# Where two normalisations and a cosine product run in a transformer layer on one NeuronCore

## The reference

```python
x = x + _layernorm(_L0_attn_ref(_layernorm(x), Wq, bq, Wk, bk, Wv, bv, Wo, bo))
x = x + _layernorm(_L0_ffn_ref(_layernorm(x), gate_w, up_w, down_w, gate_s, up_s, down_s))
# attention: 32 heads of 16 channels; queries and keys get a rotary embedding,
# q * cos + rotate_half(q) * sin, twice (position and coarse time); causal softmax
# feed-forward: down((silu(gate(x) * gate_s) * (up(x) * up_s))) * down_s, 1408 wide, ternary weights
```

## Time and profile before

| What | Value |
|---|---|
| time, median of 3 runs | 2977.47 us (2976.86 to 2978.34) |
| time of the profiled execution | 2972.66 us |
| its span, from first to last instruction | 2970.9 us |
| mean granted clock of PE | 0.961 |
| busy in the span: PE, DVE, ACT, POOL | 2555.1, 2219.8, 1325.7, 1034.1 us |

### The profile page before, as it was taken

One profiled execution on the slowest core, in us unless ns is written; L12 is line 12 of the kernel. 1 busy time (PEld: TensorE's weight loads), 2 busy tenths in 40 slices (PEclk: granted clock), 3 DMA queues, 4 the chain that ended last, 5 costly groups with the idle time before them and its releaser, 6 DMA issues. The chain is left out here.

```text
span 2970.9 us, 58497 instructions
## 1 busy us (share of the span) xinstructions
PE 2555.1 (86%) x19584; PEld 1229.0 (41%) x19584; DVE 2219.8 (75%) x6495; ACT 1325.7 (45%) x1710; POOL 1034.1 (35%) x1051
## 2 busy tenths in 40 slices
PE   3788888888888888888888888708999999999997
PEld 1344443444443444434444444204444444444443
DVE  5899899889898898898898999573554555455544
ACT  2465555556555555555555555432222222222221
POOL 3456365365464663653654655210000000000000
PEclk9999999999999999999999999859999999999999
DMA  4232332332332323323323323040111111111111
GB/s 151 85 88 76 97 105 74 110 98 73 105 93 74 109 73 99 105 70 112 100 72 105 99 68 108 30 177 15 43 71 42 56 42 71 42 56 48 65 42 43
DMA packets 125363, 237.31 MB, mean 80 GB/s; under 512 B 11440, under 2 KB 94896, under 8 KB 111920
## 3 DMA queue, kind: packets, MB, share of 16 engines
q1 hardware_dynamic: 123056, 232.84, 24.8%
q10 hardware_dynamic: 2048, 1.05, 0.1%
HBM read 148.39 MB, written 84.41 MB: 78 GB/s over the span
## 5 line engine op out<-in xcount | busy, mean ns | idle before, releaser
L674 DVE CUSTOM_DVE_ANT_0 mx<-mx,causal 128x512 f32<-128x512 f32 (+3 forms) x2048 | 942.9, 517 | 99.5 <-PE mx L799 98.6
L518 ACT ACTIVATE probs<-ts,exp_scale 128x1024 f32<-128x1024 f32 x640 | 713.1, 1114 | 656.5 <-PE ts L813 536.1
L444 POOL TENSOR_SCALAR_AFFINE_SELECT probs<-probs 128x512 f32<-128x512 f32 x512 | 326.3, 655 | 691.0 <-ACT probs L518 691.0
L1219 DVE SCALAR_TENSOR_TENSOR hidden<-gu,up_scale,silu 128x512 f32<-128x512 f32 x176 | 131.9, 749 | 417.9 <-PE gu L1269 408.0
L1078 ACT ACTIVATE silu<-gu,gate_scale 128x512 f32<-128x512 f32 x176 | 121.0, 688 | 631.2 <-PE gu L1269 631.2
L1053 POOL TENSOR_TENSOR f_rstd<-f_var,f_neg_half 128x4 f32<-128x4 f32 x32 | 32.3, 1010 | 929.1 <-DVE f_var L1196 647.5
L799 PE MATMUL mx<-kT,qT 64*128 64x512 f16 (+3 forms) x2048 | 256.1, 308 | 69.5 <-issue 51.2
L1267 PE MATMUL gu<-f_xT_hi,gate_hi 128*128 128x512 f16 x704 | 267.9, 381 | 52.0 <-issue 52.0
L827 PE MATMUL xb<-probs,vs 128*32 128x512 f32 (+3 forms) x4096 | 308.8, 443 | 1.6 <-POOL probs L444 1.1
L674 DVE DVE_READ_ACCUMULATOR2_ANT row_max<- 128x1 f32 x2048 | 282.9, 138 | 0.0
L1269 PE MATMUL gu<-f_xT_lo,gate_hi 128*128 128x512 f16 x704 | 267.8, 380 | 0.0
(11 more groups left out here) (145 smaller groups left out, 4493.2 us busy)
## 6 DMA issues: line engine op xcount, KB each, us to landing
slots<-half SPq DMA_DIRECT2D x260, 128.0 KB, 12.8
qT<-slots SPq DMA_DIRECT2D x128, 256.0 KB, 3.9
kT<-slots SPq DMA_DIRECT2D x128, 256.0 KB, 3.9
xn<-x SPq DMA_DIRECT2D x16, 1024.0 KB, 4.8
xr<-x SPq DMA_DIRECT2D x16, 1024.0 KB, 5.4
slots<-half SPq DMA_DIRECT2D x256, 64.0 KB
x<-xr SPq DMA_DIRECT2D x16, 1024.0 KB, 5.7
f_xn<-x SPq DMA_DIRECT2D x16, 1024.0 KB, 4.8
```

The costliest lines, as they stand in the source:

```text
L444: nc.gpsimd.affine_select(out=d, in_=d, compare_op=ALU.is_ge, fill=0.0, base=0, pattern=[[0, HG], [1, P]], channel_multiplier=-1).then_inc ...
L518: nc.scalar.activation(probs[:, g % 2, u, :, :], ts[:, :, :], ACT.Exp, scale=exp_scale[:, 0:1]).then_inc(ts_read, 1)
L674: last = nc.vector.tensor_tensor_reduce(out=scores, in0=scores, in1=causal[:, T - P * (qt + 1):T], scale=1.0, scalar=-3e38, op0=ALU.add, o ...
```

## The change

The normalisations of both layer norms move from DVE to ACT. ACT computes scale * in + bias with one value per partition, so the mean enters as an offset: DVE writes minus the mean beside the variance, and POOL, behind the inverse root and a wait on it, multiplies the two into `offset`. ACT's first normalisation of a sequence waits for that. The normalisations stand at the end of ACT's part of the same steps as before on DVE. The cosine product moves from DVE to POOL, behind the two sine products and a wait on the second, ahead of the sum; it waits, as before, for the buffer of `roped` to be read.

```diff
-        COSINE_AT = later(0, 0)
 # POOL
-            def inverse_root(i, ready, v, out, done):
+            def inverse_root(i, ready, v, out, done, minus_mean, offset, offset_done):
                 pool.wait_ge(ready, i + 1)
                 nc.gpsimd.tensor_tensor(out, v, neg_half[:, :], ALU.pow).then_inc(done, 1)
-                return done, i + 1
+                pool.wait_ge(done, i + 1)
+                nc.gpsimd.tensor_tensor(offset, minus_mean, out, ALU.mult).then_inc(offset_done, 1)
+                return offset_done, i + 1
...
                 pool.wait_ge(turned_done, 8 * i + n + 1)
+                cosine(i, n)
+
+            def cosine(i, n):
+
+                b = n % 2
+                wait_if_any(pool, qk_lo, 8 * i + n - 1)
+                nc.gpsimd.tensor_tensor(roped[:, b, :], biased[:, b, :], cos_sb[:, :], ALU.mult).then_inc(cosine_done, 1)
 # ACT
+            def normalise_x(i, t):
+                if t == 0:
+                    act.wait_ge(offset_ready, i + 1)
+                nc.scalar.activation(xn[:, t, :], xn[:, t, :], ACT.Identity, bias=offset[:, t:t + 1],
+                                     scale=rstd[:, t:t + 1]).then_inc(xn_ready, 1)
+
+            def normalise_projected(i, t):
+                if t == 0:
+                    act.wait_ge(offset1_ready, i + 1)
+                nc.scalar.activation(y[:, t, :], y[:, t, :], ACT.Identity, bias=offset1[:, t:t + 1],
+                                     scale=rstd1[:, t:t + 1]).then_inc(projected_normed, 1)
...
+                    if exists(i + 1) and (not isinstance(i, int) or i >= 0):
+                        for t in NORMALISE_AT.get(s, ()):
+                            normalise_x(i + 1, t)
+                    if exists(i - 1):
+                        for t in NORMALISE1_AT.get(s, ()):
+                            normalise_projected(i - 1, t)
+
+            for t in range(NT):
+                normalise_x(0, t)
 # DVE: cosine, normalise_x and normalise_projected go, with their places in body; in both variances
+                nc.vector.tensor_scalar(minus_mean[:, :], mv[:, :, 0], -1.0, None, ALU.mult)
                 nc.vector.tensor_scalar(var[:, :], mv[:, :, 1], EPS, None, ALU.add).then_inc(var_ready, 1)
```

More of the change, by code:

```diff
@@ L129, in attention_phase @@
         rstd = sb("rstd", [P, NT])
+        minus_mean = sb("minus_mean", [P, NT])
+        offset = sb("offset", [P, NT])
         stats1 = sb("stats1", [P, NT, 6])
@@ L133, in attention_phase @@
         rstd1 = sb("rstd1", [P, NT])
+        minus_mean1 = sb("minus_mean1", [P, NT])
+        offset1 = sb("offset1", [P, NT])
         mx = pb("mx", [P, 4, T])
@@ L155, in attention_phase @@
         rstd_ready = sem("rstd_ready")
+        offset_ready = sem("offset_ready")
         xn_ready = sem("xn_ready")
@@ L195, in attention_phase @@
         rstd1_ready = sem("rstd1_ready")
+        offset1_ready = sem("offset1_ready")
         projected_normed = sem("projected_normed")
@@ L472, in body @@
                     if s == VARIANCE_AT + 1 and exists(i + 1) and (not isinstance(i, int) or i >= 0):
-                        before = inverse_root(i + 1, var_ready, var[:, :], rstd[:, :], rstd_ready)
+                        before = inverse_root(i + 1, var_ready, var[:, :], rstd[:, :], rstd_ready,
+                                              minus_mean[:, :], offset[:, :], offset_ready)
                     if s == VARIANCE1_AT + 1 and exists(i - 1):
-                        before = inverse_root(i - 1, var1_ready, var1[:, :], rstd1[:, :], rstd1_ready)
+                        before = inverse_root(i - 1, var1_ready, var1[:, :], rstd1[:, :], rstd1_ready,
+                                              minus_mean1[:, :], offset1[:, :], offset1_ready)
                     if exists(i - 1):
@@ L478, in body @@
                             before = residual(i - 1, t)
-            inverse_root(0, var_ready, var[:, :], rstd[:, :], rstd_ready)
+            inverse_root(0, var_ready, var[:, :], rstd[:, :], rstd_ready,
+                                              minus_mean[:, :], offset[:, :], offset_ready)
             pool.wait_ge(largest_ready, 1)
@@ L646, in low_of_attention @@
                                         ALU.subtract).then_inc(aT_ready, 1)
[L648 to L652, removed]
             def low_of_roped(i, n):
@@ L717, in variance_of_projected @@
                 await_step(out_step, (NT + 1) * (i + 1))
+                nc.vector.tensor_scalar(minus_mean1[:, :], mv1[:, :, 0], -1.0, None, ALU.mult)
                 nc.vector.tensor_scalar(var1[:, :], mv1[:, :, 1], EPS, None, ALU.add).then_inc(var1_ready, 1)
[L720 to L724, removed]
             def body(i):
@@ L736, in body @@
                             shift_of_maxima(i + ahead, n // NU)
-                    if s in COSINE_AT and exists(i + COSINE_AT[s][1]):
-                        cosine(i + COSINE_AT[s][1], COSINE_AT[s][0])
                     if u == 3 and exists(i + (g - 1) // NG):
@@ L750, in body @@
                             variance_of_x(i + 1)
-                        for t in NORMALISE_AT.get(s, ()):
-                            normalise_x(i + 1, t)
                     if exists(i - 1):
@@ L757, in body @@
                             variance_of_projected(i - 1)
-                        for t in NORMALISE1_AT.get(s, ()):
-                            normalise_projected(i - 1, t)
             dve.wait_ge(consts, 7)
@@ L765, in _ @@
             largest_weight(0)
-            for t in range(NT):
-                normalise_x(0, t)
             for n in range(1, 4):
```

## The result

The changed kernel takes 3043.86 us (median; 3042.17 to 3058.00), the kernel before 2977.16 on the same chip: a ratio of 1.0234 (of the means of the runs; the medians make 1.0224), with a 95% interval of 1.0203 to 1.0264. The change is slower by 66.7 us, where the prediction said 53.5. The profiled execution took 3043.86, with a span of 3042.1; against the 2972.66 of the profile before that is 71.2 more.

What follows compares the result with a forecast made beforehand. The prediction took POOL to bound steps 25 to 33 already. Its terms, 48 + 4.5 + 1 = 53.5 us, gave 3026 us on the profiled execution and 3031 on the median; range 2955 to 3070.

Steps and rivals of the forecast that it cites:

- its largest term: Steps 25 to 33: with four cosine products added, POOL's chain ends 3.4 us later in 14 sequences, 48 us.
- these nine steps: Bias of n=2 (step 25) to rope sum of n=5 (step 33): 28.7 us, POOL busy 27.35 to 27.48.
- The relief: Steps 25 to 33: POOL's sine products, inverse root and residual additions get back 2.0 us a sequence (bounds 0 and 3.7).
- a slack of 0.4: End of step 33: ACT takes up POOL's sum 0.52 us late, absorbing 0.4 us of the chain's growth.
- n=0: Rope at step 17: sum 0.57 us late for ACT, half reaching PE, 0.3 × 15 = 4.5 us (bounds 0 and 9).
- n=6: This tile's rope: its lateness falls on a wait DVE ends and its relief pays back, zero.
- Steps 6 to 9: ACT's four normalisations of x push step 7's exponential 1.7 us, but PE waits anyway: zero (bounds -1.0 and +1.7).
- The cover: Steps 27 to 29: ACT's normalisations delay exponentials by up to 2.8 us, hidden by POOL's lateness; otherwise 39 us.
- (a): Rival, chance 0.15: DVE is the bound, POOL's growth is absorbed, PE's waits shrink; 53 us faster, 2924 us.
- (b): Rival, chance 0.17: ACT becomes a second bound at steps 6 to 9 with its whole 1.7 us; 26 more, 3057.
- (c): Rival, chance 0.08: no change, 2977; POOL's full relief leaves 1.7 a sequence, repaid by step 9 and DVE's waits.
- What was to be seen: Signs: steps 25 to 33 take 31 to 35 us, ACT's waits grow at n=3 and n=5, DVE loses 170 us.

## Why the prediction was right

**The forecast.** The sum came to four fifths of what was measured, and the place and the size of its largest term were right. That the time fell into the range says less, since a range of 2955 to 3070 held kernels faster than the one before too.

**The bound.** "POOL is the bound of these nine steps already" held in the direction that counted, and was half of the truth. What is added to a full row costs its whole length (+3.4; the price is gone with the row shortened). But I had read "an engine that never rests" as one engine's own work, with DVE's 27.89 us of 28.69 in the same row of the window: the move of the residual additions, with POOL at 21.5, left the length at 28.4. Two full engines in one window mean that work added to either costs, and work taken from one returns little.

**The row's terms.** Four cosines at 1.27 and the 0.08 between neighbours held. One line of the changed kernel each (ns, minimum/median/maximum), against the earlier trace rows:

```profile
L440 POOL TENSOR_TENSOR roped<-biased,cos_sb x128: 1263/1274/1664, 49.4 to 1909.0; 128x512 f32<-128x512 f32 x128
...
L430 POOL TENSOR_TENSOR turned<-biased,sin_sb x128: 1260/1268/1755, 46.7 to 1905.9; 64x512 f32<-64x512 f32 x128
...
L422 POOL TENSOR_TENSOR offset<-minus_mean,rstd x32: 202/203/204, 10.4 to 2008.2; 128x4 f32<-128x4 f32 x32
...
L420 POOL TENSOR_TENSOR rstd<-var,neg_half x32: 1011/1022/1063, 9.3 to 2007.1; 128x4 f32<-128x4 f32 x32
...
L521 ACT ACTIVATE xn<-xn,offset,rstd x64: 799/810/820, 10.6 to 1803.0; 128x512 f32<-128x512 f32 x64
...
L466 POOL TENSOR_TENSOR xr<-xr,projected x64: 1256/1271/1713, 278.2 to 2013.0; 128x512 f32<-128x512 f32 x64
```

The relief came as forecast: the medians of the first sine product (1516 to 1268), the inverse root (1278 to 1022) and the residual addition (1452 to 1271) fell to their old minima. The offset took 0.20 and about 0.1 of waiting, where I had 0.4. 5.4 + 0.3 less the 3.4 by which the row grew makes the relief 2.3, against my 2.0. Of the 3.8 by which the chain was to grow, 3.4 were to remain behind a slack of 0.4; the row grew by 3.4, and steps 26 to 35 show 3.34, so there was hardly any slack. That the 3.4 was met so closely is luck: 0.4 less growth and 0.3 less slack cancel.

**n=0.** 0.3 a sequence predicted. ACT waits 0.64 us for this sum, near the 0.57 of the prediction, and step 19 is longer by 0.76; but by step 25 all of it but 0.08 has come back. In the two kernels with the cosines outside the row alone it is 0.07 and 0.08 as well. The half that was let through was a guess, and too much.

**n=6, the step that failed.** "For n=6 the same lateness falls on a wait that DVE ends today and that its relief pays back: zero." It cost +0.95 in step 4, of which 0.37 came back in step 5, and +0.88 to 1.13 in step 4 of each other kernel with this cosine on POOL. The wait that DVE ends is the low half of attention, and it stands behind ACT's copy of the transposed tile, which stands behind the high half of n=6 on ACT: the chain begins at POOL, and DVE's relief comes too late in it. PE's 2.09 us above are its end; over eleven sequences that wait grew from a mean of 1.20 to 1.81. In PE's timeline before it reads:

```profile
1028.70 0.23 PE L785 MATMUL xb<-w_hi,xT_hi 128*128 128x128 f16 x1 [1.20 <-DVE aT_lo L645]
```

**Steps 6 to 9, taken as zero.** ACT's normalisations did push the exponential of step 7: step 6 grew by 1.60, near the bound of 1.7, because two normalisations, 1.52 together, stand between ACT's DMA issues and that exponential. Steps 8 and 9 gave 1.2 back. With n=6 and small terms steps 4 to 10 cost 1.29. Over 14 or 15 sequences the profiles' 71 are so about 47 for the row (48 forecast), 1 for n=0 (4.5), 19 for steps 4 to 10 (0: the mis-sized term), and 5 for steps 36 to 38, behind the stretch at the low clock, and what follows them (not named).

**The cover.** "POOL's lateness covers this. Without that cover it would cost 14 × 2.8 = 39" is wrong in its reason. With the normalisations on ACT and the additions out of POOL's row, the kernel takes 2963.04, against 2962.70 without the normalisations. The exponentials of steps 26 and 27 are later by 2.0 us there too, but step 29 gives 2.7 back. What pays, by PE's waits, is DVE, relieved of 4.2 us: the wait for the division, 2.52 in the kernel with the move alone (its timeline), is absent with the normalisations on ACT, while that for the low half of attention in step 30 grows from a mean of 0.42 to 1.89.

```profile
1085.88 1.11 PE L860 MATMUL xb<-ident,attn 128*128 128x128 f32 x4 [2.52 <-DVE attn L699]
```

**The rivals.** (a) fell as it stood: its condition was that relief and slack exceed 5.8 us on POOL, and they made under 3. The move of the additions then made room of about that size, and with the four cosines the gain was 24 us over the kernel before, not 53. (b) named the right place and size in step 6 but not the return in steps 8 and 9. (c) counted on step 9's payment, of which 0.78 came, and on 1.7 in the row, which grew by twice that.

**What was to be seen.** The row at 31 to 35 with POOL nearly always busy, the wait for the division replaced, the sine product at 1.26: all there. ACT's waits grew at n=5 (from a mean of 0.67 to 3.80 over the eleven sequences), hardly at n=3 (1.53 to 1.83), which the prediction had named beside it. DVE's busy time fell by 148, where I had 170.

## What to carry to other kernels

Before work is moved to an engine with a low average share, take the stretch between the two events that the others wait for, and read all engines' busy time in it: an engine at 95% there has no room, whatever its share of the span, and a second one at 97% says that relieving the first will not pay either. Then ask not only which engine, but when: the same four products cost 47 us in a full row and nothing once four additions, whose result is not wanted there, had moved to where the engine idles. A wait whose releaser has just been relieved can still begin at the engine that was loaded, so follow it back past its last releaser.

## What the runs showed of the hardware

Beside POOL's products two kinds of DVE's instructions with operands in SBUF lasted two to two and a half times their own length: two residual additions took 3.44 us beside sine products against 0.68 each alone, two normalisations, with one tensor operand each, 2.64 against 0.54 each. I had counted this for POOL's relief, and not for the normalisations in the kernels that put a cosine beside them. By the Trainium skill, page "SBUF — State Buffer", section "Who interferes with whom", a DVE instruction with two inputs in SBUF, as the addition is, and a GpSimd instruction that reads SBUF exclude each other, each for its whole length, and a `tensor_scalar`, as the normalisation is, can do so too. The 3.44 us agree with that: the two sine products end at 1109.53 and 1111.20, the two additions at 1110.08 and 1111.75, each 0.55 behind a product.
